# Attention between two small expert layers, 8 cores: twenty slots' probabilities transposed by TensorE, separate places for the last output quarters, and the first loads issued ahead of the branch

## The reference, cut to what matters

```
x = x + 0.5 * FFN(LN(x))
x = x + ATT(LN(x))
x = x + 0.5 * FFN(LN(x))

FFN(u):  probs = softmax(u @ gate.T); top 2, renormalised -> combine (T, 8)
         out = sum_e combine[:, e] * (u @ A[e].T) @ B[e].T * 2
ATT(u):  q, k, v = u @ wq, u @ wk, u @ wv       (16 heads of 128, rotary on q and k)
         s = q k^T / sqrt(128), keys p with p <= t and p > t - 1024
         out = softmax(s) v @ wo
```

## Time and profile before

| | |
|---|---|
| runs, lowest / median / highest | 1611.07 / 1617.13 / 1626.21 us |
| the profiled execution, its own time | 1613.93 us |
| its span, slowest core (core 2, share 0) | 1612.4 us |
| cores, shortest to longest span | 1588.5 to 1612.4 us |
| busy: PE, DVE, ACT, POOL | 1389.4, 904.3, 700.6, 398.5 us |
| the 16 DMA engines, queue of SP (q1) / of POOL (q0) | 58.0% / 25.5% of the span |
| HBM read, written | 155.34 MB, 65.60 MB |

### The profile page before, as it was taken

One profiled execution on the slowest core, in us unless ns is written; L12 is line 12 of the kernel. 1 busy time (PEld: TensorE's weight loads), 2 busy tenths in 40 slices (PEclk: granted clock), 3 DMA queues, 4 the chain that ended last, 5 costly groups with the idle time before them and its releaser, 6 DMA issues.

```text
span 1612.4 us, 30681 instructions; the slowest of 8 cores (1588.5 to 1612.4 us)
## 1 busy us (share of the span) xinstructions
PE 1389.4 (86%) x8674; PEld 734.1 (46%) x8836; DVE 904.3 (56%) x1860; ACT 700.6 (43%) x1428; POOL 398.5 (25%) x797
## 2 busy tenths in 40 slices
PE   2678799999999899988999999835999899898983
PEld 2333344444444444444555555422555555555541
DVE  5562334565564631444677777722566777777752
ACT  4554312222212124335555556532666655656541
POOL 0011203213112112011114444541111333433321
PEclk8789899999999999999999999956999999999996
DMA  9989926999999579679999999998899999999851
GB/s 269 308 236 219 192 71 176 179 166 189 178 180 181 131 203 323 153 146 170 183 191 199 191 192 196 208 231 162 158 209 201 216 185 200 192 200 200 175 140 73
DMA packets 502012, 305.20 MB, mean 189 GB/s; under 512 B 431664, under 2 KB 441904, under 8 KB 499536
## 3 DMA queue, kind: packets, MB, share of 16 engines
q1 hardware_dynamic: 447792, 171.73, 58.0%
q0 software_dynamic: 41376, 106.23, 25.5%
q10 hardware_dynamic: 12672, 25.17, 5.5%
HBM read 155.34 MB, written 65.60 MB: 137 GB/s over the span
## 4 chain that ended last, share of the span: by engine, by line
PE 52%; SPq 15%; DMA 12%; issue 9%; DVE 6%; ACT 4%; POOL 1%; DVEq 0%; ACTq 0%; POOLq 0%
PE ps_all L488 26%; SPq L1749 14%; PE ps_all L726 9%; DMA work<-work 6%; PE ps_all L592 5%; PE ps_all L681 3%; PE ps_all L645 3%; DMA w<-wk 2%; ACT work L1325 2%; DMA work<-xu 1%; PE ps_all L741 1%; PE ps_all L425 1%; DVE stat L820 1%; DMA w<-wv 1%; DVE xu L1074 1%
## 5 line engine op out<-in xcount | busy, mean ns | idle before, releaser
L488 PE MATMUL ps_all<-w,work 128*128 128x512 bf16 x2253 | 519.6, 386 | 11.4 <-ACT work L1156 3.8
L1030 DVE TENSOR_REDUCE nm<-ps_all 128x1 f32<-128x1024 f32 (+7 forms) x288 | 292.3, 1017 | 171.9 <-PE ps_all L656 154.5
L488 PEld LDWEIGHTS ps_all<-w,work 128*128 128x128 bf16 x2304 | 227.1, 99 | 287.2 <-issue 29.8
L1325 ACT ACTIVATE work<-ps_all,nm 128x1024 bf16<-128x1024 f32 (+7 forms) x224 | 215.6, 963 | 204.9 <-DVE nm L1030 181.4
L726 PE MATMUL ps_all<-w,work 128*128 128x512 bf16 x1101 | 283.9, 386 | 18.6 <-DVE work L907 9.2
L592 PE MATMUL ps_all<-w,work 128*128 128x512 bf16 x1109 | 267.0, 384 | 5.6 <-ACT work L1311 1.7
L681 PE MATMUL ps_all<-w,work 128*128 128x128 bf16 x1856 | 140.4, 223 | 62.7 <-POOL work L1595 33.5
L681 PEld LDWEIGHTS ps_all<-w,work 128*128 128x128 bf16 x1856 | 121.6, 100 | 101.5 <-issue 70.6
L592 PEld LDWEIGHTS ps_all<-w,work 128*128 128x128 bf16 x1152 | 108.2, 99 | 118.3 <-issue 10.1
L726 PEld LDWEIGHTS ps_all<-w,work 128*128 128x128 bf16 x1152 | 106.0, 99 | 120.0 <-issue 26.4
L1594 POOL TENSOR_TENSOR work<-work,mwt_sb 128x128 bf16<-128x128 bf16 x160 | 68.9, 431 | 311.9 <-DMA work<-work 253.4
(11 more groups left out here) (90 smaller groups left out, 1440.7 us busy)
## 6 DMA issues: line engine op xcount, KB each, us to landing
tab<-x_ext SPq DMA_DIRECT2D x72, 256.0 KB, 4.6
y<-work POOLq DMA_DIRECT2D x72, 256.0 KB, 4.3
xu<-x_ext SPq DMA_DIRECT2D x15, 1024.0 KB, 6.7
xu<-wq SPq DMA_DIRECT2D x13, 1024.0 KB, 8.4
w<-wk ACTq DMA_DIRECT2D x12, 1024.0 KB, 10.5
w<-wv ACTq DMA_DIRECT2D x12, 1024.0 KB, 9.0
unT_s<-work POOLq DMA_DIRECT2D x18, 512.0 KB, 5.6
kT_s<-work POOLq DMA_DIRECT2D x72, 128.0 KB, 2.5
```

Source lines behind the costliest of these rows:

```text
L488: i = e.matmul(K.bank(kv_bank(r)), K.unT[t % G][:, c * 128:(c + 1) * 128], K.w(w, qd, c), start=(c == 0), stop=(c == NCH - 1))
L1030: e.reduce_max(K.nm[:, n % 4:n % 4 + 1], reg[:, 0:128 * len(kv)], axis=AX, negate=True).then_inc(S.a_max, 1)
L1325: e.activation(p[:, 0:w], K.ps[:, (n % 2) * 1024:(n % 2) * 1024 + w], AF.Exp, bias=K.nm[:, n % 4:n % 4 + 1], accum_out=K.sums[:, n % 16:n ...
```

## The change

It has four parts.

1. **Twenty slots through TensorE.** `tp_slots` are slots 8(NQ-1) to 8(NQ+1)+3: the last tile of b1, the first tile of b2 and half of the second. Their probabilities are no longer transposed by a DMA. `pe_p` multiplies each block with the identity into PSUM bank 5 (blocks 1 to 4) and bank 6 (blocks 5 to 8), right behind the scores of two slots later; ACT copies bank 5 to `K.pT` (`act_p`), DVE bank 6 (`dve_p`, for full tiles alone). Banks 5 and 6 are those of the q projection before and of the output projection after. The twenty slots use three buffers of `K.p`, and all slots behind them too.
2. **Places for y.** The quarters of the last tile but one and of the last have places of their own in `work` (`y_place`), six more than before, so that the adds don't wait for a store.
3. **The end woven anew.** Quarters 1 to 3 of the last tile but one all come at the end of step NQ+1, ahead of the last tile's layer norm transposes, where they lay between them before; of the last tile's layer norm and its transposed copy, DVE now does half (`dve_ln3_last`, `dve_x3_last`) and ACT half.
4. **First instructions ahead of the branch.** SP's three first loads, POOL's `eps`, `gA` and `bs`, and ACT's first exponential stand ahead of the register load and the branch. What follows them in the branch is unchanged, SP's wait for the first tile too.

```diff
+def tp_slots(R):
+    return range(8 * (R.NQ - 1), 8 * (R.NQ + 1) + 4)
+def two_banks(R, n):
+    return len(tile_of(R, n // 8)[2]) > 4
...
 def p_slot(K, R, n):
-    n1 = 8 * (R.NQ + 2)
-    if n < n1:
+    tp = tp_slots(R)
+    if n < tp[0]:
         return K.p[n % 5], K.t_p[n % 5], n // 5
-    return K.p[(n - n1) % 3], K.t_r[(n - n1) % 3], (n - n1) // 3
+    if n in tp:
+        return K.p[(n - tp[0]) % 3], None, None
+    k = n - tp[-1] - 1
+    return K.p[k % 3], K.t_r[k % 3], k // 3
+def p_free(e, K, R, n):
+    tp = tp_slots(R)
+    _, sem, k = p_slot(K, R, n)
+    if n in tp:
+        j = n - tp[0]
+        if j < 3:
+            e.wait_ge(K.t_p[j], 16 * count(tp[0], j, 5))
+        else:
+            p_transposed(e, K, R, j - 2)
+    elif k >= 1:
+        e.wait_ge(sem, 16 * k)
+    elif n > tp[-1]:
+        p_transposed(e, K, R, len(tp))
...
+def pe_p(e, K, R, n):
+    S = K.S
+    if n not in tp_slots(R):
+        return
+    k, nb = n - tp_slots(R)[0], len(tile_of(R, n // 8)[2])
+    p, _, _ = p_slot(K, R, n)
+    if k == 0:
+        e.wait_ge(S.q_ev, 4 * R.NQ)
+    e.wait_ge(S.a_exp, n + 1)
+    if k >= 1:
+        e.wait_ge(S.p_ev5, k)
+    for b in range(min(nb, 4)):
+        m = e.matmul(K.bank(5, b * 128, b * 128 + 128), p[:, b * 128:(b + 1) * 128], K.id_sb[:],
+                     start=True, stop=True)
+    m.then_inc(S.p_mm5, 1)
+    if nb > 4:
+        if tp_wide(R, k):
+            e.wait_ge(S.p_ev6, tp_wide(R, k))
+        for b in range(4, nb):
+            m = e.matmul(K.bank(6, b * 128 - 512, b * 128 - 384), ...)
+        m.then_inc(S.p_mm6, 1)
...
             pe_scores(e, K, R, a, h)
+            pe_p(e, K, R, 8 * a + h - 2)          # DVE: dve_p behind dve_max
...
+            act_p(e, K, R, 8 * a + h - 2)         # ACT: ahead of act_exp
             act_exp(e, K, R, a, h)
...
+def act_p(e, K, R, n):
+    ...
+    pT = p_place(e, K, R, n)
+    e.wait_ge(S.p_mm5, n - tp_slots(R)[0] + 1)
+    e.activation(pT[:, 0:w], K.bank(5, 0, w), AF.Copy).then_inc(S.p_ev5, 1)
+def dve_p(e, K, R, n):
+    ...
+    e.tensor_copy(pT[:, 512:512 + w], K.bank(6, 0, w)).then_inc(S.p_ev6, 1)
...
 def sp_p(e, K, R, a, h):
+    if n in tp_slots(R):
+        return
...
     if c0 == 0:
         e.wait_ge(K.ld_wo[qd], 64)
+        if g < 2:
+            p_evicted(e, K, R, len(tp_slots(R)))
...
+def y_place(K, R, n):
+    j, s = divmod(n, 4)
+    if j < R.NQ - 2:
+        return K.ys[s % 2], n // 2
+    if j == R.NQ - 2:
+        return K.yl[s], n // 2 if s < 2 else 0
+    return K.yl[4 + s], 0
...
+            if h == 7 and i == R.NQ + 1:
+                dve_ln3_last(e, K, R)
+                for s in range(1, 4):
+                    dve_y_out(e, K, R, R.NQ - 2, s)
...
-def sp_phase_a(e, K, R):
+def sp_first(e, K):
     e.dma_start(out=K.xu[0][:], in_=K.xd[0]).then_inc(S.ld_x0, 16)
     e.dma_start(out=K.id_sb[:], in_=K.idd[:]).then_inc(S.ld_id, 16)
     e.dma_start(out=K.xu[1][:], in_=K.xd[1]).then_inc(S.ld_x1, 16)
+def sp_phase_a(e, K, R):
     e.wait_ge(S.ld_x0, 16)
     load_piece(e, K, 0)
...
+            sp_first(e, K)
             each_role(e, K, program)
```

More of the change, by code:

```diff
@@ L180, in __init__ @@
         self.ys = [v(7936 + 1024 * j, 1024).bitcast(F32) for j in range(2)]
+        self.yl = self.ys + [v(20480 + 1024 * j, 1024).bitcast(F32) for j in range(2)]
+        self.yl += [v(1024 * j, 1024).bitcast(F32) for j in range(4)]
         self.unTB = [v(10240 + 2048 * j, 2048) for j in range(2)]
@@ L686, in pe_av @@
     x.then_inc(S.av_mm, 1)
+def pe_p(e, K, R, n):
[14 more added lines that the diff above has]
+    if nb > 4:
+        if tp_wide(R, k):
+            e.wait_ge(S.p_ev6, tp_wide(R, k))
+        for b in range(4, nb):
+            m = e.matmul(K.bank(6, b * 128 - 512, b * 128 - 384), p[:, b * 128:(b + 1) * 128],
+                         K.id_sb[:], start=True, stop=True)
+        m.then_inc(S.p_mm6, 1)
 def pe_phase_b1(e, K, R):
@@ L738, in pe_x3 @@
     e.wait_ge(S.x3_ap, j + 1)
+    if j == R.NQ - 1 and x == 1:
+        e.wait_ge(S.x3_apd, 1)
     region_free(e, K, R, n)
@@ L750, in pe_gate_b @@
     region_free(e, K, R, n)
-    e.wait_ge(S.x3_ev, 2 * j + 2)
+    if j < R.NQ - 1:
+        e.wait_ge(S.x3_ev, 2 * j + 2)
+    else:
+        e.wait_ge(S.x3_ev, 2 * j + 1)
+        e.wait_ge(S.x3_evd, 1)
     out = region(K, n + 1)[:, 0:GAW]
@@ L796, in pe_phase_b2 @@
                 pe_gate_b(e, K, R, i - 3, n)
-            if y4 and h in (1, 3, 5):
+            if y4 and h in (1, 3, 5) and i != R.NQ + 2:
                 pe_y_b(e, K, R, i - 4, h // 2 + 1)
@@ L904, in dve_y_out @@
     e.wait_ge(S.y_mm, 4 * F + s + 1)
-    if n >= 2:
-        e.wait_ge(K.st_y[n % 2], 16 * (n // 2))
-    e.tensor_add(K.ys[n % 2], K.xu[j % 2][:, s * 512:(s + 1) * 512],
+    out, before = y_place(K, R, n)
+    if before:
+        e.wait_ge(K.st_y[n % 2], 16 * before)
+    e.tensor_add(out, K.xu[j % 2][:, s * 512:(s + 1) * 512],
                  K.bank(6 - s % 2)).then_inc(S.y_add, 1)
@@ L1039, in dve_rcp @@
     e.reciprocal(K.rcp[:, c:c + 4], K.sums[:, c:c + 4]).then_inc(S.a_rcp, 1)
+def dve_p(e, K, R, n):
+    S = K.S
+    if n not in tp_slots(R) or not two_banks(R, n):
+        return
+    w = 128 * (len(tile_of(R, n // 8)[2]) - 4)
+    pT = p_place(e, K, R, n)
+    e.wait_ge(S.p_mm6, tp_wide(R, n - tp_slots(R)[0] + 1))
+    e.tensor_copy(pT[:, 512:512 + w], K.bank(6, 0, w)).then_inc(S.p_ev6, 1)
 def dve_phase_b1(e, K, R):
@@ L1067, in dve_o @@
         for j in (3, 4):
-            e.wait_ge(K.t_p[j], 16 * count(8 * (R.NQ + 2), j, 5))
+            e.wait_ge(K.t_p[j], 16 * count(tp_slots(R)[0], j, 5))
     if i >= 2:
@@ L1088, in dve_ln3, with dve_ln3_last, dve_x3_last @@
                            ALU.mult).then_inc(S.ln_var, 1)
+def dve_ln3_last(e, K, R):
+    S = K.S
+    j = R.NQ - 1
+    L = 2 * R.NT + j
+    e.wait_ge(S.ln_nm, j + 1)
+    e.wait_ge(S.x3_mm, 2 * j)
+    e.tensor_scalar(K.x3[:, 1024:2048], K.xu[j % 2][:, 1024:2048], K.rstd[L % 2][:, 0:1],
+                    K.nmr[:, 0:1], ALU.mult, ALU.add).then_inc(S.x3_apd, 1)
+def dve_x3_last(e, K, R, n):
+    S = K.S
+    j = R.NQ - 1
+    e.wait_ge(S.x3_mm, 2 * j + 2)
+    e.wait_ge(S.g_mm, R.NT + j)
+    e.tensor_copy(K.x3T[:, 1024:2048], region(K, n + 1)).then_inc(S.x3_evd, 1)
 def dve_phase_b2(e, K, R, own):
@@ L1108, in dve_phase_b2 @@
                 dve_rcp(e, K, 2 * a)
-            if h in (1, 3, 5) and y4:
+            if h in (1, 3, 5) and y4 and i != R.NQ + 2:
                 dve_y_out(e, K, R, i - 4, h // 2 + 1)
+            if h == 1 and i == R.NQ + 2:
+                dve_x3_last(e, K, R, 8 * a + h)
             if h == 3 and f3:
@@ L1327, in act_exp, with p_place @@
                  accum_out=K.sums[:, n % 16:n % 16 + 1]).then_inc(S.a_exp, 1)
+def p_place(e, K, R, n):
+    e.wait_ge(K.S.av_mm, (n - PTB) // 2 + 1)
+    return K.pT[n % PTB]
+def act_p(e, K, R, n):
+    S = K.S
+    if n not in tp_slots(R):
+        return
+    w = 128 * min(4, len(tile_of(R, n // 8)[2]))
+    pT = p_place(e, K, R, n)
+    e.wait_ge(S.p_mm5, n - tp_slots(R)[0] + 1)
+    e.activation(pT[:, 0:w], K.bank(5, 0, w), AF.Copy).then_inc(S.p_ev5, 1)
 def act_av(e, K, R, quad):
@@ L1401, in act_phase_b2 @@
             n = 8 * a + h
-            if h < 2 and f3:
+            if f3 and (h == 0 or h == 1 and i - 3 < R.NQ - 1):
                 act_x3(e, K, R, i - 3, h, n)
@@ L1691, in pool_st_y @@
     e.wait_ge(K.S.y_add, 4 * (R.NT + i) + s + 1)
-    e.dma_start(out=K.yd[i][:, s * 512:(s + 1) * 512], in_=K.ys[n % 2]).then_inc(K.st_y[n % 2], 16)
+    e.dma_start(out=K.yd[i][:, s * 512:(s + 1) * 512], in_=y_place(K, R, n)[0]).then_inc(K.st_y[n % 2], 16)
 def pool_oT(e, K, R, i):
@@ L1737, in pool_phase_b2 @@
                 pool_oT(e, K, R, i)
-            if h == 0 and 0 <= i - 4 < R.NQ:
-                pool_st_y(e, K, R, i - 4, 0)
-            if h in (2, 4, 6) and 0 <= i - 4 < R.NQ:
+            if h % 2 == 0 and 0 <= i - 4 < R.NQ and i != R.NQ + 2:
                 pool_st_y(e, K, R, i - 4, h // 2)
+            if h == 7 and i == R.NQ + 1:
+                for s in range(4):
+                    pool_st_y(e, K, R, R.NQ - 2, s)
     for s in range(2):
```

46 lines of the change are left out of this document (34 added, 12 removed).

## The result

| | before | after |
|---|---|---|
| time, median of all runs | 1618.12 us (6 runs) | 1643.95 us (6 runs) |
| fastest run | 1611.07 | 1597.70 |
| ratio of the compared runs, first measurement | | 0.9885, 95% interval 0.9837 to 0.9933 |
| the same, measured again with more runs (`after_again`, below) | | 0.9939, 0.9909 to 0.9968 |
| forecast | | 1587 (1570 to 1604) |

The kernel is faster. By how much is not as sure: 1597.7 us in the first measurement (two runs), a mean of 1605.6 in the second (nine). Both intervals hold 0.991 to 0.993, some 11 to 15 us.

The account below looks back on a forecast made before the run. The prediction took share 0 to set the time and its gap between q and output projection to be bound by DMA time, with latency on top. Gap -24, start -1, end -5 made -30 us: 1587 us, range 1570 to 1604.

Parts of the forecast that it names:

- The gap of share 0, -24: Core 2, q projection to output projection: 50 us in place of 74, as transposes leave the full DMA engines.
- The forecast's own sign of being wrong: Share 0's first output projection past 1095 us with DMA still full would show that the loads hold the gap.
- the loads keep the gap: Rival for share 0's gap: DMA stays full with the `wo` loads; only -10 there, time 1602, chance 0.16.
- by engines alone 1074: Early end for share 0's gap: output projection at 1074 if engines alone decide, -34 us.
- Full slot 2.7 us, short slot 1.3 us: Twenty slots through TensorE: time per slot, DVE being the fullest engine of a full one.
- lockstep: Rival in the twenty slots: single bank 5 chains transposes, copies and exponentials, 5.5 to 6.5 us per full slot; chance 0.03.
- The wait ends with it and costs nothing more: Share 0, slot 136: ACT's wait for slot 135's buffer ends with TensorE's product with V, adding nothing.
- Share 1, -38 in the gap: Core 3, q projection to output projection: gap some 62 us instead of 100; share 1 ends at 1556, not the slowest.
- the DMA term of that sum (58): Core 3's gap by DMA time: 100 - 42 = 58 us, with 20480 of 29339 packets gone.
- Start, -1: First loads ahead of the branch: even core's tile asked for some 1.5 us earlier, -1 us, between 0 and -2.
- End, -5: Last adds and stores: two waits go, last stores land slightly slower; -5 us, between -3 and -7.
- The page on transposes: Transposes as fast as regular DMAs would save 10 us of share 0's DMA time, not 20; the trace spoke against it.

Follow-up runs that it names:

- after_again: The changed kernel itself, with no further edit, measured again against the kernel before: ratio 0.9939, mean span of the four even cores (even mean) 1595.9 us.
- e4_o_early: The changed kernel with POOL's load of the first stored o tile issued in stage 0 of the second phase instead of stage 1: ratio 0.9898 against the kernel before.
- e8_o_before: The kernel before with only the first stored o tile loaded in stage 0 of the second phase: ratio 1.0007, gap 66.4 us instead of 73.0.
- e3_first: The kernel before with only the first loads, the eps memset and the table load issued ahead of the branch: ratio 0.9990.
- e9_no_first: The changed kernel with early o load, reordered slot buffers and first loads back behind the branch: ratio 0.9861 against the kernel before.
- e2_end: The kernel before with only places for the last two tiles' quarters, their new order and the split last norm: ratio 0.9959.

## Why the forecast was right in kind and too large

- **The gap of share 0, -24: the step that failed.** The forecast saw that the load of o is issued last and that TensorE is kept until it lands, and then put that landing at 1084 without following POOL's queue: ahead of the last piece of `wo` and of that load stands a store that waits for a DMA transpose of the last o of b1. The trace of before had it: on core 2, which the forecast read, the store waited 12.32 us and TensorE 6.39 us for the load behind it. On the even cores read, the projection began at 1084 to 1101, and -24 became -12. With the load moved (e4_o_early) the gap is 51.4 us against the 50 forecast, and first L821 came at 1079.2 to 1094.6 against 1083. But that is the size of the forecast with an edit which it didn't have: by the profiles 6.6 us of it come from the early load alone (e8_o_before), and the slots give 12 us of gap behind the late load and 15 behind the early one, with errors of 3 to 4, not 24. The order of the queue is the part of the shortfall that the runs show; the rest of the DMA arithmetic was too large or is lost in the other wait. The forecast's own sign of being wrong, the first output projection past 1095 with the DMA still full, came on three of the six even cores read. The rival "the loads keep the gap" (-10) named the right size. Its reason, that POOL issues one piece per step of `wo` and waits in between, is nearer than the forecast's, but it is one order in a queue, not the volume. (Two slips of the forecast change nothing: "by engines alone 1074" should be the 1076 that its steps add up to, and the chances for a gain of over 1% add up to 0.85.)
- **Full slot 2.7 us, short slot 1.3 us: near.** From slot 136's exponential at 1047.6 core 4 has all eight full slots, eight short ones and the six up to the projection ahead of it, 8 x 2.7 + 10 + 8 = 40 us by the forecast's figures, and is through at 1084.4, after 36.8. By its exponentials a full slot takes 2.4 us and a slot of one block 1.5. No lockstep. But at 1047 the forecast had four of the full ones done, which the next point explains.
- **"The wait ends with it and costs nothing more": wrong.** It held ACT up for 4.7 to 10.7 us and TensorE for 4.6 to 5.3 (1.4 on core 6 of after_again). The forecast looked only at TensorE's own next product; the exponentials of all slots behind 136 stand on ACT behind the wait, and nothing of the twenty could begin. Moving it to slot 138 took most of TensorE's wait away; the 2.9 us of gap and 3.0 of even mean that came with it lie within the scatter.
- **Share 1, -38 in the gap: right** (100 to 60 on the cores read, 98 to 61 on the mean), and as said it does not set the time. Its packets came out cheaper than the forecast's 2.04 ns (1.24 on core 5), so that the DMA term of that sum (58) agrees in part by luck; the other term, 22 slots at 2.7 us (59), doesn't need it.
- **Start, -1: right in its nil effect, wrong in its sign at the first piece.** The forecast put the gate loads (1.06 MB, not 2) behind the first tile before and beside it after. They stood 0.6 us behind it before (3.14 against 2.56 on core 2) and 0.5 after. The tile landed at nearly the same time; the first piece went out 4 to 6 us later on even cores, since SP itself went on later, and ACT's second table load took 1.3 us more. e3_first: +0.7, with an error of 3. Odd cores were put at 5 to 13 us earlier at the first piece; they ask between 17.4 and 18.6, from 15.2 to 24.5 before (15.4 to 16.3 in e9_no_first). Their q projection begins 5.5 us earlier in after_again (760.5 against 766.0 on the mean), near the 5 that were counted.
- **End, -5: right**, -4.1 in e2_end's even mean, with an error of 2.
- **What was given back.** Of the 12 us of gap and 4 of the end, the spans show 9.5. The q projection began 5 us later in after_again's profile than in that of before (644.4 against 639.5 on the mean of the even cores), 0.3 later on cores 4 and 6 of the first profile of after. Among all kernels this mark lies between 639.5 and 648.2, and single cores between 633 and 657, also between kernels with the same first stage; this scatter, whose cause was not looked for, is as large as the smaller parts of the change.
- **The page on transposes.** By the Trainium skill, "Advanced Engine Details and Errata", section X-Bar Transpose (TRN2), they would be as fast as regular transfers, and the gap would have kept 10 us more of DMA time. The 1.97 ns per packet of core 4 after the change speak against it as the 2.04 before did: a full slot of 1024 packets takes 2.0 us, plain loads 0.637 x 66 / 11.97 = 3.5 us per MB, 0.9 for the same 256 KB. Core 5's 1.24 ns, 1.3 us against 0.86 for its own loads, are nearer to the page and still dearer than it says.

## What to carry to other kernels

When an edit makes the work ahead of a point faster, list for that point every input, and for each the queue that issues it and all waits ahead of it in that queue; the second latest input is the new bound, and moving its issue may be worth as much as the edit (here 8 us beside 10). Where DMA engines are full, don't count a small transfer whose data come late by its bytes alone: here twelve small transposes, on three buffers, cost 13.7 us for 4 us of DMA time. A buffer rotation that is changed at a boundary should hand out first the buffer that has been free longest (here it took a wait of up to 5.3 us off TensorE, though no time that these runs resolve). To see whether a load came late, look at every engine that waits for it: here SP went on late, while DVE had long had the tile.
